# Transfers of turned maxima issued by ScalarE, and loads of x three batches ahead, in a decoder block on one core

## Chip, core and metric

One core of a Trainium2 chip. The metric is the device time of one execution in microseconds, lower is better. The core has TensorE (PE, its weight loads PEld), VectorE (DVE), ScalarE (ACT), GpSimd (POOL) and SyncE (SP). DMAs issued by SP or ACT stand in that engine's own instruction stream: it does nothing else while it issues one, and it waits in order.

## What is computed

A decoder block in three parts, each followed by a layer norm, for 16 batches of 256 tokens with 256 features:

```python
x = _layernorm(x + _L0_attn_ref(x, A, B, W, b))                 # u = x B^T; h = scan(A, u); h W^T + b
x = _layernorm(x + _L0_xattn_ref(x, ctx, ctx, Wq, ..., bo))     # 16 heads of 16, rope, window of 50
x = _layernorm(x + _L0_ffn_ref(x, router_w1, router_w2, w1, w2, w3))  # 16 experts, each takes its top 64 tokens
```

The first is a linear recurrence over the sequence, the second attention on a context (keys and values come from `ctx`) in which a query sees the keys at most 50 positions away, the third a mixture of experts.

## The kernel before

`mixing` does the first two parts for one batch after another and the router's first product; `routing` picks the tokens; `experts` runs the experts. The change is in `mixing` alone.

**Passes.** All engines run a software pipeline of passes, written as `step(it)`, with `it.i` from -2 to 17. A pass works on the heads of batch i, on the K, V and Q projections and x1 transposition of batch i + 1, on the recurrence (U, scan, Y) of batch i + 2, and on output projection, layer norm and router product of batch i - 1 or i - 2 (`DELAY`). Four passes are unrolled in a hardware loop, and the first and last ones are written out. `there(it, name)` says whether the batch exists.

**Head slots.** Within a pass TensorE goes through t = 0..15. Slot t computes the scores of head t (`heads`), then the scores once more with keys in the partitions for head t - 9 (`turned_heads`, `LAG`), so that the softmax needs no transposition of the probabilities. That second product subtracts the row maxima: they stand as one more row, `TOP`, of `q_stack`. Between them lie the other products: X transposition at t = 0, K at 1, Q at 3, the output projection O at 4 and 7, U at 5, Y at 8, V at 11, OX (transposition of x2) at 13, the router product R at 15. The products with the probabilities (`gather`) run at t = 2, 6, 10, 14 for one group of four heads.

**Maxima.** DVE writes the negated row maxima of each group of four heads into `nmax`. At t = 1, 5, 9, 13 TensorE transposes those of a group that is complete (`turn_maxima`, L469), ACT copies them to `nmaxT` (`keep_maxima`, L630, counted in `nmax_kept`), and SP moves them with two transfers of 2 KB in all into row `TOP` of `q_stack` (`maxima`, L281). The turned product of the first head of the group waits for them in `nmax_in` (L480): the group turned at t = 1, 5, 9, 13 is needed at t = 5, 9, 13 and at t = 1 of the next pass.

**SP's queue in a pass.** In this order: the load of x for batch i + 2 (`xin` and `xT`, two buffers each), the load of `cT`, the maxima of the groups -1 and 0, the transfers that lay out K and Q of batch i + 1 as stacks (`stack`: high and low halves, 24 transfers), with the maxima of the groups 1 and 2 between them, and the store of x2. Each waits for its producer, and what stands behind it waits too.

**POOL's queue in a pass.** One `inverse_sums` (three operations, L383 to L388), then `xb` = x + bias (L402), which waits for `x_in`, then `cosine(0)`, `rotate(0)`, `cosine(1)` (L358, L365: the rotation of K and Q), `inverse_sums`, `rotate(1)`, `lower` twice, and the rest. DVE multiplies with each inverse (`attnT`, L790) at t = 2, 6, 10, 14, and it scans U into `state` (L802) at t = 6 behind that product. Y at t = 8 needs `state`.

**ACT's queue.** At t: `keep_maxima` if due, then the exponentials of head t - 9 (L619, into `probsT`), which TensorE waits for two slots later since there are two banks; then the copies out of the shared banks (`raw_k`, `x1T` at t = 1 and 2, `raw_q` at 4, `x2T` at 14, R at 15), `high` of K and Q at 5 and 7, and the logs and exponentials for sums and deviations.

Of the kernel before, what the change touches and what calls it, by code (L numbers as in the profile page):

```python
# [20 lines left out]
F32 = mybir.dt.float32  # L21
# [15 lines left out]
HG = 4  # L37
NG = NH // HG
# [39 lines left out]
def counts(value):  # L78

    return not isinstance(value, int) or value > 0  # L80
# [23 lines left out]
def mixing(nc, dram, keep):  # L104
# [5 lines left out]
    with ExitStack() as ctx:  # L110
        def sb(name, *shape, dt=F32):
            return ctx.enter_context(nc.sbuf_tensor(name, [P, *shape], dt))
# [4 lines left out]
        def sem(name):  # L117
            return ctx.enter_context(nc.semaphore(name))
# [32 lines left out]
        TOP = 2 * STACK  # L151
        q_stack = [sb(f"q_stack{n}", 2, NH // 2, S, dt=F32R) for n in range(2)]
# [4 lines left out]
        nmaxT = [sb(f"nmaxT{n}", P, dt=F32R) for n in range(2)]  # L157
# [20 lines left out]
        fixed_set = sem("fixed_set")  # L178

        ORDER = (("X", "Q", "U", "Y", "OX"), ("K", "O", "V", "R"))  # L180
        ready, freed = ({n: sem(f"{what}_{n}") for names in ORDER for n in names} for what in ("ready", "freed"))
        FREED_EARLY = {"OX": 1, "R": 1}
        xb_ready = sem("xb_ready")
# [10 lines left out]
        nmax_turned, nmax_kept = sem("nmax_turned"), sem("nmax_kept")  # L194
        nmax_in = [sem(f"nmax_in{n}") for n in range(2)]
# [9 lines left out]
        FIXED = 4 + 2 + NG  # L205
# [8 lines left out]
        def uses(it, name, before=0):  # L214

            return it.lin(1, 1 - DELAY[name] - before)

        def there(it, name):

            return it.batch(-DELAY[name])  # L220
# [14 lines left out]
        def group(t, lag):  # L235

            return (t - lag) // HG

        def has(it, n):

            return it.batch(0) if n >= 0 else it.batch(-1)

        @block.sync
        def _(sp):
            def load_x(par, b):
                sp.dma_start(xin[par][:], dram["x"][b].rearrange("(t p) d -> p t d", p=P)).then_inc(x_in[par], 16)
                sp.dma_start(xT[par][:], dram["xT"][b].rearrange("(k p) s -> p k s", p=P)).then_inc(x_in[par], 16)

            def load_c(par, b):
                sp.dma_start(cT[par][:], dram["cT"][b].rearrange("(k p) s -> p k s", p=P)).then_inc(c_in[par], 16)  # L250

            sp.dma_start(wb[:], weight("mix_BT")).then_inc(const_in["wb"], 16)
            load_x(0, 0)
            sp.dma_start(ww[:], weight("mix_WT")).then_inc(const_in["ww"], 16)
            load_c(0, 0)
            sp.dma_start(wk[:], weight("WkT")).then_inc(const_in["wk"], 16)
            sp.dma_start(cos[:], dram["cos"]).then_inc(const_in["rope"], 16)
            sp.dma_start(sin[:], dram["sin"]).then_inc(const_in["rope"], 16)
            sp.dma_start(wq[:], weight("WqT")).then_inc(const_in["wq"], 16)
            load_x(1, 1)  # L260
            sp.dma_start(wv[:], weight("WvT")).then_inc(const_in["wv"], 16)
            sp.wait_ge(wo_zeroed, 1)
            for q in range(HG):
                sp.dma_start(wo[32 * q:32 * q + DH, :, :], wo_rows[q]).then_inc(const_in["wo"], 16)
            sp.dma_start(wo[DH:DH + 1, 0, :], dram["bo"].partition_broadcast(1)).then_inc(const_in["wo"], 16)
            sp.dma_start(rw1[:], weight("rw1")).then_inc(const_in["rw1"], 16)
            sp.wait_ge(fixed_set, FIXED)

            def met():

                sp.sem_inc(sp_met, 1)

            def maxima(it, g):

                if has(it, g):
                    sp.wait_ge(nmax_kept, it.lin(NG, g + 1))
                    met()
                    par = (it.r + (g < 0)) % 2
                    f = 2 * (g % NG)
                    for a in range(2):  # L280
                        sp.dma_start(q_stack[par][TOP:TOP + 1, a, f:f + 2, :].bitcast(F32),  # L281
                                     nmaxT[g % 2][HG * a:HG * a + HG, :].bitcast(F32)).then_inc(nmax_in[g % 2], 16)

            def stack(it, half, which, kind):

                part, landed = (high, high_ready) if kind == "high" else (low, low_ready)
                par = (it.r + 1) % 2
                sp.wait_ge(landed[which], it.lin(1, 2))
                met()
                f = slice(4 * half, 4 * half + 4)  # L290
                for c in range(3):
                    if PARTS[which][c] == kind:
                        for a in range(2):
                            rows = slice(STACK * a + DH * c, STACK * a + DH * c + DH)
                            dst = q_stack[par][rows, a, f] if which else k_stack[par][rows, f]
                            p = 64 * a + 32 * half
                            src = part[which][p:p + 32].rearrange("p f s -> p (f s)")
                            sp.dma_start(dst.rearrange("d (k f) s -> d k (f s)", f=KT).bitcast(F32),
                                         src.bitcast(F32)).then_inc(stacked[half][which], 16)

            def step(it):
                if it.batch(2):
                    if it.at_least(0):
                        sp.wait_ge(ready["V"], uses(it, "V", 1))
                        met()
                        sp.wait_ge(xb_ready, it.lin(1, 1))
                        met()
                        load_x(it.r % 2, it.lin(1, 2))
                    load_c(it.r % 2, it.lin(1, 2))
                maxima(it, -1)  # L310
                maxima(it, 0)
                if there(it, "K"):
                    if it.at_least(1):
                        sp.wait_ge(scoreT_ready, it.lin(NH, -NH // 2))
                    stack(it, 0, 0, "high")
                    stack(it, 0, 0, "low")
                    stack(it, 0, 1, "high")
                maxima(it, 1)
                if there(it, "Q"):
                    stack(it, 0, 1, "low")  # L320
                    if it.at_least(1):
                        sp.wait_ge(scoreT_ready, it.lin(NH, 0))
                    stack(it, 1, 0, "high")
                    stack(it, 1, 0, "low")
                maxima(it, 2)
                if there(it, "Q"):
                    stack(it, 1, 1, "high")
                    stack(it, 1, 1, "low")
                if there(it, "O"):
                    sp.wait_ge(x2_ready, it.lin(1, -1))  # L330
                    sp.wait_ge(ready["OX"], uses(it, "OX"))
                    met()
                    sp.dma_start(dram["x2"][bass.ds(it.lin(S, -2 * S), S), :].rearrange("(t p) d -> p t d", p=P),
                                 x2cur[:]).then_inc(x2_kept, 16)

            for i in (-1, 0, 1):
                step(Iter(0, i, 4))
            with sp.Fori(0, 3) as j:
                for r in (2, 3, 4, 5):
                    step(Iter(j, r, 4))  # L340
            for i in (14, 15, 16, 17):
                step(Iter(0, i, 4))
            sp.wait_ge(x2_kept, 16 * NB + 1)

# [250 lines left out]
        def _(act):  # L595
# [27 lines left out]
            def keep_maxima(it, t):  # L623

                g = group(t, 5)
                if has(it, g):
                    act.wait_ge(nmax_turned, it.lin(NG, g + 1))
                    if counts(it.lin(16 * NG, 32 * (g // 2))):
                        act.wait_ge(nmax_in[g % 2], it.lin(16 * NG, 32 * (g // 2)))
                    nc.scalar.copy(nmaxT[g % 2][0:2 * HG, :], attn[g % 2][0:2 * HG, S:S + P]).then_inc(nmax_kept, 1)  # L630

            def invert_sums(it, t):

                g = group(t, 16)
                if has(it, g):
                    act.wait_ge(sums_ready, it.lin(NG, g + 1))
                    nc.scalar.activation(sums_log[:], sums[g % 2][:], ACT.Ln).then_inc(sums_log_ready, 1)
                    act.wait_ge(sums_log_ready, it.lin(NG, g + 1))
                    nc.scalar.activation(rough[g % 2][:], sums_log[:], ACT.Exp, scale=-1.0).then_inc(rough_ready, 1)  # L639
# [749 lines left out]
```

## Time and profile before

| | |
|---|---|
| median of 3 runs | 1241.02 us (1233.14 to 1242.78) |
| profiled execution | 1240.79 us, span 1239.0 us |
| TensorE busy over the span | 1058.1 us (85%) |
| DVE, ACT, POOL busy | 668.3, 542.9, 667.4 us |
| DMA | 117.18 MB, 95 GB/s in the mean |

The first stage ends near 570 us, the routing near 600, and the experts take the rest. TensorE's granted clock is told as a share of full speed. In a timeline, "[1.18 <-DMA q_stack<-nmaxT]" at the end of a row says that the engine had been idle for 1.18 us and that the landing of this transfer ended it.

### The profile page before, as it was taken

To read this page: it belongs to the slowest core of one execution; us is meant where nothing else is said; L and a number is where in the kernel's file an instruction comes from. 1 tells how busy PE (TensorE), PEld (TensorE's weight loads), DVE (VectorE), ACT (ScalarE), POOL (GpSimd) and SP (SyncE) were. 2 spreads that over 40 slices of the span, in tenths; PEclk is the share of its full clock that TensorE was granted. 3 is DMA by queue.
4 is the path that set the end of the run, shared out by engine and by line. 5 is a ranking of instruction groups with operands and counts; after the bars stand their busy time and mean duration, and the time that the engine had idled before them with its cause. 6 is when DMAs were issued, how large, how long until landed. Compare 5 with 4: busy or idle time off the path is not lost. (4 is left out here: it accounts for less than half of the span.)

```text
span 1239.0 us, 22698 instructions
## 1 busy us (share of the span) xinstructions
PE 1058.1 (85%) x6564; PEld 886.8 (72%) x6564; DVE 668.3 (54%) x2184; ACT 542.9 (44%) x1179; POOL 667.4 (54%) x808
## 2 busy tenths in 40 slices
PE   5679888889889988875079999999999999999990
PEld 4567777667767776653068888888888888888880
DVE  5557666666667666641743444544354454444437
ACT  1245444444545444542044445545444454454431
POOL 6356555555555556540144666566556656655543
PEclk9899999999989999987579999999999999999995
DMA  5333233233333332204133554453445445444338
GB/s 144 91 80 80 78 86 85 79 86 83 85 86 87 87 85 63 61 19 145 63 124 73 115 107 107 110 106 61 108 113 110 106 106 116 58 105 111 51 68 255
DMA packets 91201, 117.18 MB, mean 95 GB/s; under 512 B 14049, under 2 KB 66402, under 8 KB 90978
## 3 DMA queue, kind: packets, MB, share of 16 engines
q1 hardware_dynamic: 65394, 81.97, 22.1%
q0 software_dynamic: 24576, 33.57, 16.4%
q8 instruction: 42, 0.69, 0.3%
q10 hardware_dynamic: 1136, 0.51, 0.2%
q14 instruction: 53, 0.43, 0.1%
HBM read 65.41 MB, written 29.36 MB: 76 GB/s over the span
## 5 line engine op out<-in xcount | busy, mean ns | idle before, releaser
L1093 POOL DMA_INDIRECT acc_rows<-y,slots_now x128 | 209.4, 1636 | 186.6 <-ACT y L1223 164.7
L1285 DVE TENSOR_TENSOR hidden<-gate,value_bank 128x512 f32<-128x512 f32 x128 | 88.0, 687 | 253.7 <-ACT gate L1232 253.7
L737 DVE CUSTOM_DVE_ANT_0 scored<-score,band 128x178 f32<-128x178 f32 x512 | 153.0, 338 | 120.6 <-PE score L457 116.7
L619 ACT ACTIVATE probsT<-scoreT 128x356 f32<-128x356 f32 x256 | 117.7, 465 | 146.0 <-PE scoreT L485 143.2
L1232 ACT ACTIVATE gate<-gate_bank 128x512 f32<-128x512 f32 x128 | 76.5, 598 | 222.0 <-PE value_bank L1130 222.0
L1074 POOL DMA_INDIRECT rows<-x_rows,rows_now x128 | 137.1, 1071 | 60.0 <-issue 46.2
L1130 PE MATMUL y_bank<-w_hi,h_hi 128*128 128x256 f32 x512 | 146.6, 286 | 0.0
L1130 PE MATMUL y_bank<-w_hi,h_lo 128*128 128x256 f32 x512 | 144.5, 282 | 0.0
L1130 PE MATMUL y_bank<-w_lo,h_hi 128*128 128x256 f32 x512 | 144.2, 282 | 0.0
L457 PE MATMUL score<-k_stack,q_stack 96*128 96x178 f32 x512 | 127.0, 332 | 14.9 <-issue 7.9
L457 PEld LDWEIGHTS score<-k_stack,q_stack 96*128 96x128 f32 x512 | 91.2, 200 | 48.2 <-issue 20.8
L485 PE MATMUL scoreT<-q_stack,k_stack 97*128 97x356 f32 x256 | 118.7, 465 | 0.0
L483 PE MATMUL scoreT<-band_bf,ident_bf 128*128 128x356 bf16 x256 | 85.6, 334 | 32.8 <-DMA q_stack<-nmaxT 32.5
L1130 PE MATMUL gate_bank<-xT_hi,w_hi 128*128 128x512 f32 x256 | 102.7, 401 | 9.2 <-DVE xT_lo L1271 6.0
L1130 PE MATMUL value_bank<-xT_hi,w_hi 128*128 128x512 f32 x256 | 102.1, 399 | 0.0
L1130 PE MATMUL value_bank<-xT_lo,w_hi 128*128 128x512 f32 x256 | 101.9, 398 | 0.0
L1130 PE MATMUL gate_bank<-xT_lo,w_hi 128*128 128x512 f32 x256 | 101.8, 398 | 0.0
L1130 PE MATMUL value_bank<-xT_hi,w_lo 128*128 128x512 f32 x256 | 101.8, 398 | 0.0
L1130 PE MATMUL gate_bank<-xT_hi,w_lo 128*128 128x512 f32 x256 | 101.7, 397 | 0.0
L383 POOL TENSOR_TENSOR inverse<-sums,rough 128x256 f32<-128x256 f32 x64 | 47.1, 735 | 93.5 <-ACT rough L639 93.5
L1130 PEld LDWEIGHTS y_bank<-w_hi,h_hi 128*128 128x128 f32 x512 | 96.6, 189 | 0.0
L1130 PEld LDWEIGHTS y_bank<-w_lo,h_hi 128*128 128x128 f32 x512 | 96.6, 189 | 0.0
(149 smaller groups left out, 2320.6 us busy)
## 6 DMA issues: line engine op xcount, KB each, us to landing
raw<-in_w SPq DMA_DIRECT2D x48, 512.0 KB, 5.4
k_stack<-high_k SPq DMA_DIRECT2D x128, 64.0 KB, 2.2
q_stack<-high_q SPq DMA_DIRECT2D x128, 64.0 KB, 2.3
xin<-in_x SPq DMA_DIRECT2D x16, 256.0 KB, 3.0
xT<-in_xT SPq DMA_DIRECT2D x16, 256.0 KB, 3.3
cT<-in_cT SPq DMA_DIRECT2D x16, 256.0 KB, 3.6
k_stack<-low_k SPq DMA_DIRECT2D x64, 64.0 KB, 2.2
q_stack<-low_q SPq DMA_DIRECT2D x64, 64.0 KB, 2.3
```

Of the source, the lines that this page charges most:

```text
L383: nc.gpsimd.tensor_tensor(inverse[b][:], sums[b][:], rough[b][:], ALU.mult).then_inc(inverse_chain, 1)
L457: mm = nc.tensor.matmul(score[t % 2][:, q * SPAN:(q + 1) * SPAN], q_stack[par][0:TOP, t % 2, t // 2, q * P:(q + 1) * P], k_stack[par][0:TO ...
L483: nc.tensor.matmul(out, ident_bf[:], band_bf[:, k, :].unsqueeze(1).to_broadcast([P, 2, SPAN]), start=True, stop=False)
L485: nc.tensor.matmul(out, k_stack[par][0:TOP + 1, f, k * P:(k + 1) * P], q_stack[par][0:TOP + 1, :, f, k * FIRST:k * FIRST + SPAN], start=Fa ...
L619: nc.scalar.activation(probsT[g % 2][:, u % HG, :, :].rearrange("p a s -> p (a s)"), scoreT[u % 2][:, 0:2 * SPAN], ACT.Exp, scale=1.0 / DH ...
L737: op = nc.vector.tensor_tensor_reduce(scored[t % 2][:, q, :], score[t % 2][:, q * SPAN:(q + 1) * SPAN], band[:, q, :], -1.0, BIG, ALU.add, ...
L1074: nc.gpsimd.indirect_dma_start(rows[:, c, :], None, dram["x2"], bass.IndirectOffsetOnAxis(ap=rows_now[par][:, c:c + 1], axis=0)).then_inc( ...
L1093: nc.gpsimd.indirect_dma_start(dram["acc"][c], bass.IndirectOffsetOnAxis(ap=slots_now[it.r % 2][:, c:c + 1], axis=0), y[m][:], None, compu ...
L1130: mm = nc.tensor.matmul(out, a[x], b[z], start=(n == 1), stop=(n == 3 * len(pairs)))
L1232: nc.scalar.activation(gate[f % 2][:], gate_bank[f % 2][:], ACT.Silu).then_inc(gate_ready, 1)
L1285: nc.vector.tensor_tensor(hidden[f % 2][:], gate[f % 2][:], value_bank[f % 2][:], ALU.mult).then_inc(hidden_ready, 1)
```

## The change

The loads of x go three batches ahead: in pass i SP loads batch i + 3, once U and `xb` of pass i - 1 have read the buffer. The load of c stays where it is. The transfers of the maxima leave SP's queue: ACT issues them right behind the copy, after a wait for its own copy. SP's hardware loop runs two rounds and not three, with four more passes written out. All else is the same.

```diff
@@ sync
-            def maxima(it, g):
-
-                if has(it, g):
-                    sp.wait_ge(nmax_kept, it.lin(NG, g + 1))
-                    met()
-                    par = (it.r + (g < 0)) % 2
-                    f = 2 * (g % NG)
-                    for a in range(2):
-                        sp.dma_start(q_stack[par][TOP:TOP + 1, a, f:f + 2, :].bitcast(F32),
-                                     nmaxT[g % 2][HG * a:HG * a + HG, :].bitcast(F32)).then_inc(nmax_in[g % 2], 16)
-
             def step(it):
+                if it.batch(3):
+                    sp.wait_ge(ready["U"], uses(it, "U", 1))
+                    met()
+                    sp.wait_ge(xb_ready, it.lin(1, 2))
+                    met()
+                    load_x((it.r + 1) % 2, it.lin(1, 3))
                 if it.batch(2):
                     if it.at_least(0):
                         sp.wait_ge(ready["V"], uses(it, "V", 1))
                         met()
-                        sp.wait_ge(xb_ready, it.lin(1, 1))
-                        met()
-                        load_x(it.r % 2, it.lin(1, 2))
                     load_c(it.r % 2, it.lin(1, 2))
-                maxima(it, -1)
-                maxima(it, 0)
                 if there(it, "K"):
...
-                maxima(it, 1)
-                if there(it, "Q"):
                     stack(it, 0, 1, "low")
...
-                maxima(it, 2)
-                if there(it, "Q"):
                     stack(it, 1, 1, "high")
...
-            with sp.Fori(0, 3) as j:
+            with sp.Fori(0, 2) as j:
                 for r in (2, 3, 4, 5):
                     step(Iter(j, r, 4))
-            for i in (14, 15, 16, 17):
+            for i in range(10, 18):
                 step(Iter(0, i, 4))
@@ scalar, keep_maxima
                     nc.scalar.copy(nmaxT[g % 2][0:2 * HG, :], attn[g % 2][0:2 * HG, S:S + P]).then_inc(nmax_kept, 1)
+                    act.wait_ge(nmax_kept, it.lin(NG, g + 1))
+                    if it.fixed and it.i == 0 and g == 0:
+                        act.wait_ge(fixed_set, FIXED)
+                    par = (it.r + (g < 0)) % 2
+                    f = 2 * (g % NG)
+                    for a in range(2):
+                        act.dma_start(q_stack[par][TOP:TOP + 1, a, f:f + 2, :].bitcast(F32),
+                                      nmaxT[g % 2][HG * a:HG * a + HG, :].bitcast(F32)).then_inc(nmax_in[g % 2], 16)
```

## Rows read from the trace of the kernel before

**Rows 1.** Windows, TensorE: stretch, length, busy time, granted clock, DMA share, GB/s
```profile
100.00:500.00 400.00, 350.62 (x2472) 0.97 0.31 81
180.00:185.00 5.00, 5.00 (x33) 0.66 0.32 79
```

**Rows 2.** Waits of TensorE from 100 to 500 us: total us, times, longest
```profile
PE scoreT L483 <- DMA q_stack<-nmaxT: 23.8, 22, 2.4
PE work L515 <- DVE state L802: 16.5, 11, 2.4
```

**Rows 3.** Waits of TensorE from 0 to 575 us
```profile
PE scoreT L483 <- DMA q_stack<-nmaxT: 32.5, 27, 2.8
PE work L515 <- DVE state L802: 23.5, 15, 3.2
```

**Rows 4.** POOL: its wait at xb from 100 to 500 us; timeline of one pass
```profile
POOL xb L402 <- DMA xT<-in_xT: 74.5, 12, 8.0
...
170.01 1.27 POOL L402 TENSOR_TENSOR xb<-xin,b_mix 128x512 f32<-128x512 f32 x1 [7.41 <-DMA xT<-in_xT]
...
174.16 1.27 POOL L358 TENSOR_TENSOR rope_q<-raw_q,cos 128x512 f32<-128x512 f32 x1
...
176.80 0.73 POOL L388 TENSOR_TENSOR inverse<-inverse,rough 128x256 f32<-128x256 f32 x1
```

**Rows 5.** Timeline of DVE, same pass: start us, duration us, instruction
```profile
177.56 0.42 DVE L790 TENSOR_TENSOR attnT<-attn,inverse 128x256 f32<-128x256 f32 x1 [3.70 <-POOL inverse L388]
177.90 1.25 DVE L802 TENSOR_TENSOR_SCAN state<-acol,work 128x256 f32<-128x256 f32 x2
...
186.92 0.73 DVE L761 TENSOR_SCALAR x2cur<-pre_O,mv_O,rstd_O 128x256 f32<-128x256 f32 x2
```

**Rows 6.** Timeline of TensorE, same pass and the start of the next
```profile
179.30 2.90 PE L515 MATMUL work<-ww,state 128*128 128x256 f32 x8 [2.20 <-DVE state L802]
...
185.03 0.33 PE L483 MATMUL scoreT<-band_bf,ident_bf 128*128 128x356 bf16 x1
185.35 1.89 PE L515 MATMUL work<-wv,cT 128*128 128x256 f32 x8
...
188.23 0.60 PE L523 MATMUL work<-ident,x2cur 128*128 128x128 f32 x4
...
190.33 0.33 PE L483 MATMUL scoreT<-band_bf,ident_bf 128*128 128x356 bf16 x1
190.66 1.03 PE L575 MATMUL work<-x2T,rw 128*128 128x256 f32 x4
...
194.17 0.33 PE L483 MATMUL scoreT<-band_bf,ident_bf 128*128 128x356 bf16 x1 [1.18 <-DMA q_stack<-nmaxT]
```

**Rows 7.** SP: timeline of the same pass; the issues of nmaxT (min, median, max ns)
```profile
191.76 1.31 SPq L281 DMA_DIRECT2D q_stack<-nmaxT  x2
...
L281 SPq DMA_DIRECT2D q_stack<-nmaxT x128: 572/617/688, 43.8 to 539.2; - x128
```

**Rows 8.** Timeline of ACT, same pass
```profile
169.27 0.82 ACT L654 ACTIVATE raw_q<-work,bq 128x256 f32<-128x256 f32 x2
...
182.81 0.25 ACT L630 CAST nmaxT<-attn 8x128 fp32r<-8x128 f32 x1 [1.88 <-PE attn L469]
...
188.94 0.24 ACT L630 CAST nmaxT<-attn 8x128 fp32r<-8x128 f32 x1
189.08 0.80 ACT L619 ACTIVATE probsT<-scoreT 128x356 f32<-128x356 f32 x2
189.78 0.56 ACT L669 COPY x2T<-work 128x512 f32<-128x512 f32 x1
```

**Rows 9.** Issues at the start: the fifth and the last of ACT, the fifth of SP
```profile
2.78 0.48 ACTq L600 DMA_DIRECT2D ident<-in_ident  x1
3.80 1.93 ACTq L602 DMA_DIRECT2D bv<-in_bv  x1
...
2.77 0.47 SPq L250 DMA_DIRECT2D cT<-in_cT  x1
```

## Prediction

> **What bounds the kernel now.** I read the windows first. Between 100 and 500 us, some twelve passes of the first stage (the passes of the mixing and attention loop), TensorE is busy 350.62 of 400 us at a granted clock of 0.97 [rows 1]. So it is TensorE that paces the stage, and what it loses is 49.4 us of idling and a few stretches at the lower clock. The experts' stage behind it holds nothing that the change touches, so it keeps its time.
>
> Second, the waits say what ended the idling [rows 2]: 23.8 us for the transfer of the turned maxima into the query stack, in 22 waits, and 16.5 us for `state`, DVE's scan, in 11: 40.3 of the 49.4 us. Over the whole stage it is 32.5 us for the maxima and 23.5 us for the scan [rows 3]. The change aims at both, so its gross worth is read here.
>
> Third, the timeline of one pass tells why each comes late. A pass takes 400 / 12 = 33 us and has 16 head slots t = 0..15.
>
> The scan's wait begins at POOL. POOL stands at `xb` until the load of x lands, 7.41 us in this pass, 74.5 us in 12 passes [rows 4]. Behind `xb` in its queue stand the rotation of K, `rope_q` and the three steps of one `inverse`, which ends at 176.80 + 0.73 = 177.53. DVE multiplies `attnT` at 177.56, only then scans, 177.90 to 179.15 [rows 5], and TensorE starts the Y projection at 179.30 after 2.20 us of waiting [rows 6]. After this wait the eight products take 2.90 us (the V projection, of the same size, shows 1.89 at 185.35), and the granted clock from 180 to 185 us is 0.66 [rows 1]: part of that window is at the lower level, 1.2 GHz, and the engine had idled just before it.
>
> The maxima's wait begins at SP. For the third group of heads ACT has the turned maxima at 188.94 + 0.24 = 189.18 [rows 8]. SP's queue is in order and holds stack transfers of the next batch in front, so the maxima go out only at 191.76 to 193.07 [rows 7]. TensorE has then stood for 1.18 us when it goes on at 194.17 [rows 6].
>
> **The change part by part.**
>
> *Loads of x three ahead.* The same two transfers a pass leave SP at the same place, but for a batch whose first use is a whole pass later. The buffers are free (U and `xb` of the pass before have run), so POOL's wait at `xb` goes. What is late next for the scan? `rope_q` needs `raw_q`, which ACT ends at 169.27 + 0.82 = 170.09 [rows 8]. Then `rope_q` 1.27 and the three inverse steps, which took 177.53 - 175.43 = 2.1 from the end of `rope_q` (174.16 + 1.27 = 175.43) [rows 4]: ready at about 173.5, 4.0 us earlier than now. The wait is 2.2 us, so all of it is covered, with 1.8 us left. Over the stage: 16.5 us in twelve passes is 1.4 a pass, by 14.5 passes that have such a load: -20 us. The waits for the scan in the first passes, before the loads matter, stay.
>
> *The clock.* A mean of 0.97 over 400 us is 12 us of work not done [rows 1]. Stretches at the lower level follow idling, as above (2.90 - 1.89 = 1.0 us lost by that one product group), and 40.3 / 49.4 = 0.8 of the idling is of the two kinds: 9.8 us. Some stalls will remain, so I take half, -4.9, and for the whole stage -5 us.
>
> *Maxima off SP.* ACT issues two transfers right behind its copy. Taken together with their shorter path (2.6 us earlier for the group above: issued at 189.2 and not at 191.8), they land before TensorE asks in every group: at worst the second issue starts at 189.9, and from the second issue to TensorE's release took 194.17 - 192.4 = 1.8 us, so 191.7 against the 193.0 at which TensorE began to wait. -32.5 us. SP loses 8 issues a pass, about 5 us, and its stack transfers only come earlier; no wait for them is among those of rows 2.
>
> *Issuing on ACT.* This is the price. No row shows a maxima transfer issued by ACT. Nearest rows: on SP the issue of just this transfer is 617 ns in the median, 572 to 688 in 128 of them [rows 7]; on ACT other transfers take 0.48, and the last of seven 1.93 [rows 9]. I take SP's duration, since it is this transfer's shape: 1.3 us for a pair, as SP shows (1.31). ACT stands for it at t = 1, 5, 9 and 13, and behind it are the exponentials, which TensorE needs two slots later, and the copies that free banks. At t = 13: the copy ends 189.18, the pair 190.6, so the two exponentials that now run 189.08 to 189.88 run 190.6 to 191.4, the first one ending at 191.1, and `x2T` (0.56) ends at 191.95 instead of 190.34 [rows 8]. TensorE's turned scores of t = 15 stand at 190.33 and would wait until 191.15 (0.8), the router product at 190.66 [rows 6] until 192.0: 1.3 us in all.
> At t = 9: the copy ends 183.06, the pair 184.4, the exponential (0.47) 184.95; TensorE's turned scores of t = 11 are at 185.03 [rows 6]: 0 to 0.4, I take 0.2. With the scan's wait gone both move together.
> At t = 1 and t = 5 a projection of 1.89 us (K and U, the size of the V product in rows 6) stands between, which is longer than the pair: nothing.
> So +1.5 a pass, by 16: +24 us. `x2cur`, ready at 187.65 [rows 5] and used at 188.23 [rows 6], has 0.6 us of slack and comes through ACT's estimate, which is now behind the pair of t = 9; that takes part of what was won: I put +2.5 us for it.
>
> The rest costs nothing: SP's loop is two rounds with more passes written out, and SP is not what anything waits for there; the load of c for batch 1 now stands behind a wait for the first U, and its K projection is a pass later.
>
> *Sum*: -20 - 5 - 32.5 + 24 + 2.5 = -31. The profiled execution took 1240.79 us (span 1239.0), and the median shown is 1241.02, so 0.2 above it. 1240.8 - 31 = 1209.8; I forecast 1210.
>
> A rule speaks against this change. In the profile, ACT and SP issue side by side at the start, at 2.78 and 2.77, each for 0.47 or 0.48 us [rows 9], as though the other was not there. The Trainium skill (Perfetto Trace Analysis, DMA Instruction — HWDGE) says that the block that generates descriptors is shared by the two issuing sequencers and locked for exclusive use, and counts the wait for the lock in the issue's duration. By it the saving would shrink to that of the first rival below; the trace does not agree for large transfers, and shows nothing for these.
>
> **The rivals.**
>
> *A. ACT's issue waits for SP's.* SP is issuing most of the time from t = 9 to 15, with transfers of about 0.6 us. If each of ACT's issues waits for one of SP's, a pair is 2.5 us, 1.2 more, at t = 13 and at t = 9 in full: +2.4 a pass, by 15, +36 where they always meet, 1246; where they meet six times in ten, +22, 1232. Against it: rows 9. The range of prices is the same one: with ACT's 0.48 an issue, a pair is 1.0, 0.3 less at both places, -9 us: 1201.
>
> *B. The load of x hides nothing.* The scan stays late for another reason (POOL's own work, 8 large operations between `xb` and `lower`, or DVE's queue), so the 20 us and the 5 of the clock stay: 1210 + 25 = 1235. For it: the other steps of POOL are in a fixed order. Against it: POOL is idle for 7.41 us just ahead, and the 1.8 us of slack above.
>
> *C. The other side: ACT becomes the bound.* If an issue on ACT takes 1.93 us, the upper one of rows 9, a pair is 3.9, 2.6 more: 2.6 at t = 13 and t = 9, and 3.9 - 1.89 = 2.0 at t = 1 and 5: 9.2 a pass, by 15 = +138: 1348. It decides from where it eats the 31 us: 2.0 a pass, 1.0 a pair, an issue of 1.15 us; slower by over 1% from about 1.35 us. Against it: the 1.93 came behind six transfers of up to 178 KB, and the maxima (2 KB) never took over 0.69 us, though SP had issued stacks of 64 KB just before.
>
> **How the numbers follow.** The forecast 0.65, A 0.13, B 0.12, C 0.10. The likeliest one's own range is 1194 (issue at 0.48 us, -9; the whole of the clock's term, -5; -2 for the spread of runs) to 1228 (1.2 us a pass more, by 15: the cover at t = 1 or 5 missing, or A where it meets half the time). A and B end near 1232 and 1235; C lies far off and is left out, as is A where they always meet. Range 1192 to 1240. About 1% is what a measurement of this kernel can tell from no change: faster is below 1228.6, slower above 1253.4. Faster: 0.62 of the forecast, 0.04 of A, 0.04 of B = 0.70. Same: 0.03 + 0.08 + 0.08 + 0.02 of C = 0.21. Slower: 0.01 of A, 0.08 of C = 0.09.
>
> **What would show it.** In the profile after: POOL no longer waits for xT at `xb` from the fourth pass on, or this part is wrong. TensorE's wait for `state` is under 5 us between 100 and 500 us (B if it stays over 10), and its wait for the maxima's transfer under 3. ACT's issue of the maxima is 0.5 to 0.7 us (A if 1.0 to 1.3 where SP issues too, C if above). New are waits of TensorE for `probsT` and for `x2T`, about 1.3 us a pass at t = 15, and for `x2cur` below 0.5. The granted clock from 100 to 500 us is 0.98 or more. A pass is 31 us. It would be wrong if the exponentials behind a pair start much later than its end, since then all four groups cost, not two.

## The result and the profile after

| | before | after |
|---|---|---|
| median | 1240.76 us (4 runs, 1233.14 to 1242.78) | 1187.27 us (4 runs, 1182.92 to 1192.01) |
| profiled execution | 1240.79 us, span 1239.0 | 1182.92 us, span 1181.1 |
| ratio | | 0.958 (95% interval 0.952 to 0.964) |

53.5 us less, where the prediction had 31 and a lower end of 1192. The direction was right, the size too small.

TensorE's waits after, over the whole first stage and the routing's start (us in total, times, longest), answer [rows 3]:

```profile
PE scoreT L469 <- ACT probsT L605: 15.9, 35, 0.9
PE work L509 <- DVE x2cur L755: 10.1, 3, 4.8
...
PE work L561 <- ACT x2T L663: 6.2, 15, 0.7
PE work L501 <- DVE state L796: 4.6, 4, 1.5
```

The 32.5 us for the maxima's transfer are gone altogether. Of the scan's 23.5 us the 4.6 of the pipeline's filling are left. In their place stand the exponentials and `x2T`. POOL no longer waits at `xb` for a load anywhere in the stage. A pass takes 28.3 us (Y at 132.79 and at 161.09), where 31 was forecast and about 33 stood before. The timeline of a pass shows how the scan lost its wait; POOL, DVE and TensorE in turn (start us, duration us), against [rows 4 to 6]:

```profile
149.30 1.28 POOL L388 TENSOR_TENSOR xb<-xin,b_mix 128x512 f32<-128x512 f32 x1
...
154.97 1.28 POOL L344 TENSOR_TENSOR rope_q<-raw_q,cos 128x512 f32<-128x512 f32 x1 [0.68 <-ACT raw_q L648]
...
157.83 0.73 POOL L374 TENSOR_TENSOR inverse<-inverse,rough 128x256 f32<-128x256 f32 x1
...
158.93 1.25 DVE L796 TENSOR_TENSOR_SCAN state<-acol,work 128x256 f32<-128x256 f32 x2
...
161.09 1.89 PE L501 MATMUL work<-ww,state 128*128 128x256 f32 x8
```

POOL is now waiting for `raw_q` and not for x, and the scan ends at 160.18, 0.9 us before Y. The eight products of Y take 1.89 us, the full clock, where they took 2.90 in [rows 6]. At t = 13 to 15 ACT pays (ACT, the issue in its queue, then TensorE), against [rows 8]:

```profile
169.43 0.24 ACT L616 CAST nmaxT<-attn 8x128 fp32r<-8x128 f32 x1
169.70 1.33 ACTq L623 DMA_DIRECT2D q_stack<-nmaxT  x2
171.19 0.83 ACT L605 ACTIVATE probsT<-scoreT 128x356 f32<-128x356 f32 x2 [1.53 <-PE attn L488]
171.90 0.59 ACT L663 COPY x2T<-work 128x512 f32<-128x512 f32 x1
...
171.72 0.33 PE L469 MATMUL scoreT<-band_bf,ident_bf 128*128 128x356 bf16 x1 [0.72 <-ACT probsT L605]
172.55 0.70 PE L561 MATMUL work<-x2T,rw 128*128 128x256 f32 x2 [0.35 <-ACT x2T L663]
```

The exponentials start 1.5 us after the copy's end, TensorE stands 0.72 and then 0.35 us (and 0.26 at t = 11 of this pass). The profile names the gather as the releaser of ACT; ACT's own queue entry shows that it was issuing.

Last, the windows over the stage up to its final wait (length, busy time of TensorE, granted clock; the 3200 products are the same), before and after:

```profile
0.00:570.00 570.00, 471.42 (x3200) 0.94 0.30 80
```
```profile
0.00:512.80 512.80, 450.11 (x3200) 0.98 0.33 88
```

The stage is 57.2 us shorter: 35.9 us less idle (98.6 and 62.7) and 21.3 us less busy. The second part goes with the clock: (1 - 0.94) x 570 = 34 us of work not done, and (1 - 0.98) x 513 = 10. These are two single executions. How far they stand for the kernels is seen below, and it is not very far.

### The profile page after: what moved, and what is told of

Read it like the earlier page. It is cut to its first block, busy times and chain, and to the rows that moved or that the text cites. A ratio compares the mean times of both kernels' runs of the same rounds, so it can differ in the third digit from the quotient of the medians.

```text
span 1181.1 us, 22568 instructions
## 1 busy us (share of the span) xinstructions
PE 1036.4 (88%) x6564; PEld 874.2 (74%) x6564; DVE 665.4 (56%) x2184; ACT 534.9 (45%) x1179; POOL 667.2 (56%) x808
## 4 chain that ended last, share of the span: by engine, by line
PE 41%; DVE 4%; issue 3%; ACT 2%; DMA 1%; POOL 0%; ACTq 0%; DVEq 0%; SPq 0%; POOLq 0%
PE y_bank L1124 15%; PE gate_bank L1124 12%; PE value_bank L1124 12%; PE turn_bank L1134 2%; DVE w_lo L1260 2%; ACT w_hi L1192 1%; DVE hidden L1279 1%; DMA acc_rows<-y,slots_now 1%; DVE last L1303 1%; DVE stats L1310 1%; DMA raw<-in_w 0%; DVE xT_lo L1265 0%; DVE mv L1314 0%; POOL acc_rows L1087 0%; ACT y L1217 0%
## 5 line engine op out<-in xcount | busy, mean ns | idle before, releaser
L443 PE MATMUL score<-k_stack,q_stack 96*128 96x178 f32 x512 | 123.1, 323 | 6.7 <-DMA q_stack<-low_q 4.2
L471 PE MATMUL scoreT<-q_stack,k_stack 97*128 97x356 f32 x256 | 114.8, 449 | 0.0
L443 PEld LDWEIGHTS score<-k_stack,q_stack 96*128 96x128 f32 x512 | 88.2, 191 | 33.6 <-DVE nmax L731 17.2
L1217 ACT ACTIVATE y<-y_bank,weight_of 128x256 f32<-128x256 f32 x128 | 61.1, 477 | 80.8 <-PE y_bank L1124 74.8
L469 PE MATMUL scoreT<-band_bf,ident_bf 128*128 128x356 bf16 x256 | 82.5, 322 | 16.1 <-ACT probsT L605 15.9
```

Of the source, the lines that this page charges most:

```text
L443: mm = nc.tensor.matmul(score[t % 2][:, q * SPAN:(q + 1) * SPAN], q_stack[par][0:TOP, t % 2, t // 2, q * P:(q + 1) * P], k_stack[par][0:TO ...
L469: nc.tensor.matmul(out, ident_bf[:], band_bf[:, k, :].unsqueeze(1).to_broadcast([P, 2, SPAN]), start=True, stop=False)
L471: nc.tensor.matmul(out, k_stack[par][0:TOP + 1, f, k * P:(k + 1) * P], q_stack[par][0:TOP + 1, :, f, k * FIRST:k * FIRST + SPAN], start=Fa ...
L1217: nc.scalar.activation(y[m][:], y_bank[m % 2][:, 0:D], ACT.Copy, scale=weight_of[:, bass.ds(it.i, 1), CB * h + m]).then_inc(y_scaled, 1)
```

## The experiments

### Each part alone, and SP's loop alone

`x_only` is the kernel of before with

```diff
+                if it.batch(3):  # with its two waits, cut here
+                    load_x((it.r + 1) % 2, it.lin(1, 3))
...
-                        load_x(it.r % 2, it.lin(1, 2))
...
-            with sp.Fori(0, 3) as j:
+            with sp.Fori(0, 2) as j:
```

> Kernel of before with the loads of x three ahead (and so SP's loop of two rounds); the maxima stay with SP. My theory (the terms of the sum, with the clock's term whole): POOL's wait at xb gone, TensorE's wait for state 16.5 -> under 5 us between 100 and 500 us, so about -20 us, and -5 to -10 of the clock: 1211 to 1216, ratio 0.977 to 0.981. Rival 1 (the scan is late for POOL's other work): 1235 or more. Rival 2 (the loop's shape or the code alone carries the part of the gain that my sum lacks): as theory 1 and 8 us less, about 1205, with TensorE's 4 us issue waits at the loop's boundaries gone.

Measured: 1200.38 us against 1235.82 of before beside it, ratio 0.972 (0.968 to 0.976), 35 us less. The theory's direction holds, but the time is 11 us under its range. It is not the second rival either, since TensorE's issue waits stand in this profile too (7.5 us, two of them 3.5 and 3.9).

`maxima_only` is the kernel of before with `maxima` taken out of SP and ACT's two issues put in, loads and SP's loop as before.

> Kernel of before with the maxima issued by ACT; loads of x two ahead and SP's loop of three rounds as before. Theory: -32.5 for the waits, +24 for ACT's issues, -0 to -5 of the clock: 1228 to 1233. Rival (the two parts help each other, since what SP no longer issues also brings the load of x earlier): SP reaches the load of x about 2 us earlier in a pass, POOL's wait at xb falls from 6 to about 4 us a pass, and the scan's wait falls with it: 1210 to 1220. TensorE's 4 us issue waits stay under the theory and go under the rival that ACT's code or SP's shorter queue removes them.

Measured: 1204.94 us, ratio 0.976 (0.973 to 0.980), 31 us less, which is even more than the rival said. Its mechanism is seen: POOL's wait at `xb`, 74.5 us in [rows 4], is less than half of that in `maxima_only`, though no load was moved:

```profile
POOL xb L385 <- DMA xT<-in_xT: 28.9, 12, 4.7
```

And in `x_only` the wait for the maxima is less although they stay with SP. TensorE's waits up to the end of the stage, first of `x_only`, then of `maxima_only`:

```profile
PE scoreT L486 <- DMA q_stack<-nmaxT: 25.3, 21, 3.0
PE work L518 <- DVE state L805: 4.6, 4, 1.5
```
```profile
PE work L498 <- DVE state L793: 14.6, 13, 3.5
PE scoreT L466 <- ACT probsT L602: 9.4, 25, 0.9
```

So each part takes some of the other's wait: 32.5 - 25.3 = 7.2 us of the maxima's, and 23.5 - 14.6 = 8.9 us of the scan's. The reason for the second is that SP comes to the load of x earlier, as POOL's shorter wait shows. The reason for the first, that with POOL earlier the stack transfers leave SP earlier, is argued and not shown; and the maxima's wait is 28.1 us in the profile of `loop_only` below, so part of the 7.2 may be the spread of executions. That is some 16 us counted in both, and 35 + 31 less 16 is 50, near the 53.5 of both together.

`loop_only` changes nothing but SP's loop.

> Kernel of before with nothing changed but SP's loop (two rounds and eight passes written out). Theory: SP waits for others at the boundaries, so nothing: within 3 us of before, TensorE's two issue waits of 4 us stay. Rival: the loop's shape decides the fetch of instructions, the two issue waits go and the time falls by about 8 us.

Measured: 1236.95 us, ratio 1.001 (0.998 to 1.004): the loop's shape is worth nothing. But its profiled execution, 1230.72 us, the fastest of its ten, has none of the two issue waits of TensorE, 7.9 us, that stand in the profile of before. That was not the kernel, as the next pair shows.

### The same kernels again

> The kernel of before, unchanged, for a second profile. Theory (TensorE's issue waits of about 4 us come and go from one execution to the next, whatever the kernel, as the fetches of instructions fall): they may be missing here and the time is then near 1232 instead of 1240; the waits for the maxima (23.8 us) and for state (16.5) stay within 3 us. Rival (they belong to this kernel's code): the same two waits, 7.9 us, stand here too.

> The kernel of after, unchanged, on the same chip as the others of this call: 1183 to 1192, TensorE's granted clock 1.00 between 100 and 400 us in every profile if the clock follows the stalls.

Measured: `before_again` 1234.47 us (the execution that was profiled), `after_again` 1189.14 us in the median with 1193.91 for the profiled one, ratio 0.957 (0.952 to 0.962), 51.3 us under the 1240.43 of before beside it. The waits of `before_again` between 100 and 500 us are within 3 us of the first profile (22.6 for the maxima, 19.2 for `state`), as expected, and one of its two issue waits is gone. TensorE's issue waits between 100 and 500 us, of `before_again`, then of `after_again`:

```profile
PE score L457 <- issue: 3.7, 1, 3.7
```
```profile
PE score L443 <- issue: 6.4, 2, 3.3
```

The page's row of the instruction queue goes with them. In turn `after`, `before_again`, `before` (`loop_only` has 24 as well, `after_again` 42):

```profile
q8 instruction: 24, 0.39, 0.1%
```
```profile
q8 instruction: 33, 0.54, 0.2%
```
```profile
q8 instruction: 42, 0.69, 0.3%
```

Executions of one kernel have 24, 33 or 42 of these packets and with them none, one or two stalls, of 2.6 to 4.3 us; this holds in all 13 profiles of this record. In before the two end at 227.44 and 358.81 us, four passes apart, which fits the turns of the hardware loop. So the profiled executions of before (42) and after (24) differ by more than the change. Pairs of a kind are 1240.79 and 1193.91 (42 packets), -46.9, and `loop_only`'s 1230.72 and 1182.92 (24), -47.8. In the second pair the stage's window is this for `loop_only` (that of after stands above):

```profile
0.00:560.30 560.30, 470.88 (x3200) 0.94 0.30 81
```

47.5 us less in all: 26.7 less idle and 20.8 less busy. The windows of `before_again` (it ends three products early) and of `after_again`, in turn, say something else:

```profile
0.00:561.60 561.60, 462.88 (x3197) 0.96 0.30 80
```
```profile
0.00:522.80 522.80, 456.39 (x3200) 0.96 0.33 87
```

Here 32.3 us are idle time and only 6.5 busy (8 with the three products), and the stage's clock reads the same in both. One pair of profiles can't tell the clock's part. The expectation that the clock of after is 1.00 in every profile failed too: it is 0.98 from 100 to 400 us in `after_again`, with low stretches at the two issue stalls (granted 0.57 from 204 to 212 and from 323 to 331 us).

### What ACT's issues cost, and where

`double_issue` puts two more transfers of 2 KB behind each pair on ACT (whose own two are 2 KB each, not in all), `three_issues` one. Nothing on TensorE waits for them.

```diff
+                    for a in range(2):
+                        act.dma_start(spare[g % 2][TOP:TOP + 1, a, :, :],
+                                      nmaxT[g % 2][HG * a:HG * a + HG, :].bitcast(F32)).then_inc(spare_in[g % 2], 16)
```

> Kernel of after with two more transfers of the same size behind each pair on ACT, to a spare buffer (same issue, nothing waits for them on TensorE), 1.2 us more of ACT per group. Theory (ACT's stall reaches TensorE at t = 11 and t = 15 in full, and at t = 3 and 7 only past 1.89 us): +1.2 at two places and +0.5 at two more, 3.4 us a pass by 15 = +50 us over after, about 1237. Rival (a pass has slack that takes it): under +15 us.

Measured: 1269.24 us, ratio to before 1.028 (1.024 to 1.032), so 82 us over after's median of 1187.27 (80 over `after_again`'s 1189.14, on another chip). TensorE waits for `probsT` for 66.0 us, 50 more than in after. That is the 50 us of the expectation; the other 30 it did not have.

> Kernel of after with one more transfer of 2 KB behind each pair on ACT (0.6 us; the double took 1.2 us and cost 82 us, of which TensorE's waits were 3.3 us a pass and the rest went with the lower clock). Theory A (a stall costs its own length up to a point, and beyond it the granted clock falls too): waits of TensorE 1.2 us a pass more, clock 0.98 or above, +18 to 25 us over after. Theory B (every stall costs 1.6 times its length): +29 or more, and a clock of 0.97.

Measured: 1229.39 us in the median of four executions that spread from 1219.47 to 1237.90, 40 over `after_again` beside it (37 without the slowest). The ratio to before is 0.988 (0.979 to 0.996). Both cost far more than the stall that I had worked out. The waits of `three_issues` up to the end of the stage, and its windows:

```profile
PE scoreT L471 <- ACT probsT L607: 38.6, 37, 1.8
PE work L563 <- ACT x2T L668: 6.2, 16, 0.7
```
```profile
0.00:555.47 555.47, 467.50 (x3200) 0.94 0.31 82
```

Against `after` the waits for ACT are 38.6 - 15.9 = 22.7 us longer, about what theory A said (1.2 a pass is 19), but the time grew by 40, as only theory B allowed (with a clock of 0.97, where it is 0.95 from 100 to 400 us), and the busy time of the same products by 17.4. The clock is back at 0.94 in the stage. One pass shows how. Behind the two stalls the transposition of x1 takes 1.05 us, where its like, four of the same size, take 0.60 for x2 at 177.65 in this pass; from 182 to 186 us the granted clock is 0.57, so most of that stretch is at the lower level:

```profile
177.65 0.60 PE L511 MATMUL work<-ident,x2cur 128*128 128x128 f32 x4
...
181.13 0.33 PE L471 MATMUL scoreT<-band_bf,ident_bf 128*128 128x356 bf16 x1 [1.22 <-ACT probsT L607]
181.97 1.84 PE L563 MATMUL work<-x2T,rw 128*128 128x256 f32 x4 [0.35 <-ACT x2T L668]
...
184.59 1.05 PE L511 MATMUL work<-ident,x 128*128 128x128 f32 x4
```

`late_issue` is after with the same issues one slot later, behind the work that TensorE needs at once:

```diff
+            def move_maxima(it, t):          # the two issues, taken out of keep_maxima
...
                     exponentials(it, t)
+                    if t in (6, 10):
+                        move_maxima(it, t - 1)
...
+                    if t in (2, 14):         # behind raw_k, behind x2T
+                        move_maxima(it, t - 1)
```

> Kernel of after with ACT's pair of issues moved one slot back: at t = 2, behind raw_k, at 6 and 10 behind the exponential, at 14 behind x2T. Theory (the price of ACT's issues is where they stand: in front of the exponentials and x2T, which TensorE needs at once): the waits for probsT and x2T, 20 us between 100 and 500 us, fall to under 6, the maxima still land in time, and a pass is 1.0 to 1.2 us shorter: 15 to 18 us less than after, about 1170. Rival (ACT is short of time over the pass, wherever the issues stand): within 5 us of after. Second rival: the maxima land late, and waits of TensorE for their transfer come back.

Measured: 1165.29 us, ratio to before 0.939 (0.934 to 0.944), 24 us less than `after_again` beside it: it beats both kernels, and by more than the 15 to 18 that I expected. The wait for `probsT` at the turned scores, 15.9 us in after, is gone, that for `x2T` is 1.3, and no wait for the maxima came back. Timeline of ACT and then of TensorE at t = 13 to 15:

```profile
162.47 0.24 ACT L616 CAST nmaxT<-attn 8x128 fp32r<-8x128 f32 x1
162.62 0.45 ACT L605 ACTIVATE probsT<-scoreT 128x356 f32<-128x356 f32 x1
163.35 0.47 ACT L605 ACTIVATE probsT<-scoreT 128x356 f32<-128x356 f32 x1 [0.28 <-PE scoreT L471]
163.36 0.58 ACTq L628 DMA_DIRECT2D q_stack<-nmaxT  x1
163.71 0.58 ACT L668 COPY x2T<-work 128x512 f32<-128x512 f32 x1
163.97 0.59 ACTq L628 DMA_DIRECT2D q_stack<-nmaxT  x1
...
164.29 0.33 PE L469 MATMUL scoreT<-band_bf,ident_bf 128*128 128x356 bf16 x1
164.61 1.03 PE L561 MATMUL work<-x2T,rw 128*128 128x256 f32 x4
```

The first issue lies under the arithmetic that was queued before it (163.36 to 163.94, while the exponential runs until 163.82), and the second beside the copy of `x2T`. So it is not quite right that ACT "does nothing else while it issues one", as the first section has it: what it had already begun goes on, and what stands behind the issue waits. The price in `after` was one of place, not of ACT's time.

### One stall a pass, in three lengths

`stall_2`, `stall_4` and `stall_6` are `late_issue` with 2, 4 or 6 spare transfers on ACT at t = 13, ahead of the exponentials.

```diff
                         keep_maxima(it, t)
+                    if t == 13 and it.batch(0):
+                        for a in range(4):
+                            act.dma_start(spare[TOP:TOP + 1, a, :, :], ident[0:HG, :]).then_inc(spare_in, 16)
```

> Kernel late_issue with two more transfers of 2 KB on ACT at t = 13 only (to a spare buffer, from a constant), ahead of the exponentials: one stall of TensorE a pass, at t = 15, like that of after. Theory (a stall costs its length, and beyond some length the granted clock falls behind it as well): waits of about 1 us a pass, clock 1.00, +13 to 20 us over late_issue. Rival (every stall costs 1.6 times its length): +22 to 30.

> As stall_2, with four transfers. Theory: waits of 2.2 us a pass, 16 times, +35 for their length; and if the clock falls behind each, one stretch of 3.4 us at the lower level a pass, which costs 1.7 us more: +27, so +55 to 65 over late_issue and a clock of 0.94 to 0.95. Rival (length alone counts and the clock follows other things): +35 to 40.

> As stall_2, with six transfers. Theory: 3.4 us a pass of waiting, +54, and one stretch at the lower level a pass, not two: +27, so +75 to 90 and a clock of 0.94 to 0.95 again, since the stall is longer but the stretch behind it is the same. Rival (1.6 times the length at every length): +87 or more, and a clock that falls further.

Measured: 1175.97, 1202.33 and 1240.17 us, so 11, 37 and 75 over `late_issue`. They ran on another chip than it, where the kernel of before took 1236.26 and not 1240.43 us, so each of the three may be 4 us more. Stage windows of `late_issue`, `stall_2`, `stall_4`, `stall_6`:

```profile
0.00:495.80 495.80, 448.89 (x3200) 0.97 0.35 92
```
```profile
0.00:506.40 506.40, 454.03 (x3200) 0.97 0.34 90
```
```profile
0.00:534.70 534.70, 466.92 (x3200) 0.94 0.32 85
```
```profile
0.00:570.40 570.40, 484.59 (x3200) 0.92 0.30 80
```

The waits for `probsT` at the turned scores in the last two:

```profile
PE scoreT L471 <- ACT probsT L608: 17.8, 16, 1.3
```
```profile
PE scoreT L471 <- ACT probsT L608: 39.2, 16, 2.8
```

With 16 stalls of 1.1 us the stage is 38.9 us longer, 20.9 of them idle and 18.0 busy; with 16 of 2.5 it is 74.6 longer, 38.9 idle and 35.7 busy. The clock accounts for the busy part: (0.97 - 0.94), taken on each length, is 32.1 - 14.9 = 17 us, and 45.6 - 14.9 = 31 us. So in these two profiles the stalls cost nearly twice what the idle column shows. The medians say rather less for `stall_4` (37 us for 21 of idle time; its four executions have mean clocks from 0.940 to 0.951) and the same for `stall_6` (75 for 39).

My expectations were half right. `stall_4` fell short of 55 to 65, since its stalls were 1.1 and not 2.2 us long and the clock did not fall behind each one. In `stall_6` the time is at the low end of my theory, but the clock fell further, as its rival said and against my one stretch a pass. In `stall_2` the granted clock did not move and the time still grew by 11 us: in its stage 5.5 us of that are idle and 5.1 are busy time. Why the same products take 5.1 us longer at the same clock stays open.

### The clock's part over all executions

Each execution has its time and its mean granted clock over the whole span on record. (1 - clock) x span is then what it lost to the clock, an estimate that takes TensorE as busy throughout, and the rest is what stalls and work take. Means in us:

| kernel, executions | time | lost to the clock | rest |
|---|---|---|---|
| before, 7, beside `after_again` | 1241.3 | 70.7 | 1170.6 |
| `after_again`, 4 | 1189.4 | 58.2 | 1131.2 |
| `late_issue`, 4, beside it | 1166.0 | 55.6 | 1110.4 |
| before, 13, beside `x_only` | 1235.6 | 68.4 | 1167.2 |
| `x_only`, 4 | 1199.9 | 62.0 | 1137.9 |
| `maxima_only`, 4 | 1205.4 | 59.9 | 1145.5 |
| `double_issue`, 4 | 1269.9 | 89.1 | 1180.8 |
| `stall_4`, 4 | 1201.5 | 67.2 | 1134.3 |
| `stall_6`, 10 | 1240.2 | 89.9 | 1150.3 |

So of the 51.9 us between before and after on one chip, 12.5 are the clock's and 39.4 are not. Over the 33 executions of before and the 8 of after it is 11 and 38. The loss of single executions goes from 60 to 76 us before and from 53 to 62 after, which is why pairs of profiles gave 20.8 us of slower products or 8. The profiled execution of `loop_only` is no good partner: its rest, 1157.0, is the smallest of the 44 executions of before and `loop_only`.

## Why the prediction was right or wrong

**What bounds the kernel, and the two chains.** Right. The scan was late because of POOL's wait at `xb`, and the maxima because of SP's queue: with the loads three ahead the first wait falls to the filling's 4.6 us, and with ACT issuing the second is zero.

**The idle terms.** The sum had -32.5 for the maxima, -20 for the scan, +24 for ACT and +2.5 for `x2cur`: -26. Measured, term by term from [rows 3] and the waits of after: -32.5; 23.5 - 4.6 = -18.9; `probsT` 15.9 and `x2T` 6.2 - 1.3, with about 3 us more for `raw_q` and `nmaxT`, +24; `x2cur` 0 (10.0 before, 10.1 after). The slot-by-slot working of ACT's price held too: 0.2 was put for t = 11 and 0.26 is shown, 1.3 for t = 15 and 0.72 + 0.35 = 1.07 is shown.

**The step that failed is the size of two terms, the clock's and the idle sum.** The mechanism was right, the sizes were not. Without the clock the sum had -26; measured are -38 to -39 over all executions. The clock's term was put at -5; it measured -11 to -12.5. Together that is the 20 us that are missing.

*The clock's term* was less than half of what it should be. I took the loss from 100 to 500 us only, 12 us at a mean of 0.97, where the stage of before lost 34 in its profile (and 23 in that of `before_again`). And I halved it, since "some stalls will remain". In after 10 us stay in one profile and 21 in the other, so something was due for that. `stall_4` and `stall_6` show the term by itself: 16 stalls of 1.1 and of 2.5 us brought 18.0 and 35.7 us of slower products.

*The idle sum* is short by 12 or 13 us, though its named terms are right within 3. The profiles of before and after have 35.9 us less idle time, 9.9 more than the sum: 7.9 are the two issue stalls, for which it has no term, and 2.5 the wait for `x2cur`, which did not come. Those of `before_again` and `after_again` have 32.3 less, though there the issue stalls grew from 3.7 to 6.7: the maxima give 32.7, the scan 26.1 - 4.6 = 21.5, the first load of x 11.4 - 7.9 = 3.5. Only against `loop_only` is it 26.7, as forecast, and that is luck: in its profile the maxima's wait is 28.1 and there is no issue stall. The change of the rest over all executions is 3 to 7 us more than these idle times, and no profile shows what makes that up. How often each kernel has issue stalls is not known, as the packets are counted in profiled executions alone, so their part in the miss stays open.

**Rival A (ACT's issue waits for SP's).** Fell. The 128 issues of after on ACT (min, median, max ns), while SP issues its stacks, take no longer than [rows 7] show for SP:

```profile
L623 ACTq DMA_DIRECT2D q_stack<-nmaxT x128: 580/586/1182, 47.1 to 481.7; - x128
```

86 of them overlap an issue of SP, with a median of 587 ns and none over 717; the 42 others have 583.5. The largest, 1182, is the first, at 47.15 us, where SP was issuing nothing, so SP did not cause it. The Trainium skill (Perfetto Trace Analysis, DMA Instruction — HWDGE) describes a descriptor block shared by two sequencers, and a wait for its lock inside the issue's duration. The trace does not agree with a wait that would be felt: the overlapping issues are 4 ns longer in the median.

**Rival B (the load of x hides nothing).** Fell: `x_only` is 35 us faster. **Rival C (ACT becomes the bound).** Not at 586 ns an issue; `double_issue` shows that the side exists, since with four issues a group the kernel is 2.8% slower than before. It put the point where the gain is eaten at about 1.0 us more a pair. The runs leave it between `three_issues` (0.6 more, 0.988 of before) and `double_issue` (1.2 more, 1.028); a straight line between the two has it near 0.8, an estimate. Gain and price were both larger than in the sum: 51 us for 31, and 80 for 50 at 1.2 us more, of which 31 are the clock's.

**The parts are not additive.** The prediction counted each wait to its own part. For both together the two waits went as it said, but it would have been wrong for either alone: -25 for the loads against 35 measured, -8.5 for the maxima against 31.

**The spread.** The sum stood against a profiled execution with two stalls of instruction issue, which I took for part of the kernel. They come and go, in after too, and the measured medians hold a mixture.

## What to carry to other kernels

When TensorE paces a stage, price a stall on it at its length plus the slower products behind it: here 16 stalls of 1.1 us cost 1.8 times their idle time and 16 of 2.5 us 1.9 times, and of the 52 us that the change gave 12 came through the clock. Compare the busy time of the same products before and after, since the idle column alone hides it, and do it over many executions: the mean granted clock that each one has on record gives the clock's part, where pairs of profiles gave anything from 8 to 21 us. What stands behind a DMA issue on an engine waits for it (0.59 us each here): put the issue behind the work that others wait for, as the transfer had a slot to spare, and look at every queue that the same engine serves, for two late transfers on one queue that is served in order are partly one problem.

## What the hardware showed that was not expected

Two profiled executions of after, 1182.92 and 1193.91 us, differ by 11 us. The second has 42 packets in the instruction queue where the first has 24, and TensorE stands 3.1 and 3.3 us at two of the loop's turns, where in the first it does not stand at all. By the mean clocks, 0.955 and 0.949, 7.7 of the 11 us are the clock's. The Trainium skill (Runtime: NRT & Kernel Launch, Instruction fetch mechanics) says that a taken branch whose target is not in the engine's window forces a fetch. The stalls at the turns agree with it; it does not say why the same loop passes without one in other executions, and what decides that stays open.
